# A state-space stage with ScalarE's own softplus, ten products with C on GpSimd in two buffers, and some sums at the next tile's head

## The reference

```python
hs = silu(causal_conv4(x @ W_in_states.T) + conv_b)        # u in the kernel
dt = jax.nn.softplus((hs @ W_dt.T) @ W_dtproj.T + b_dtproj)
Bm, Cm = hs @ W_b.T, hs @ W_c.T
dA  = exp(-exp(A_log)[d, n] * dt[l, d])
dBu = dt[l, d] * Bm[l, n] * hs[l, d]
h[l] = dA[l] * h[l - 1] + dBu[l]                            # a scan along l
y = sum_n h[l, d, n] * Cm[l, n] + hs * D
out = (y * silu(x @ W_in_gates.T)) @ W_out.T
```

## Time and profile before

| | us |
|---|---|
| median of three runs | 3419.03 |
| the runs | 3418.29 to 3426.33 |
| span of the profiled execution | 3415.4 |
| first scan of the state-space stage | 54.54 |
| last product of the stage ends | 1884.6 |
| pitch of a batch, from step 0 to step 0 | 113.7 |

### The profile page before, as it was taken

How to read it: one execution, slowest core, us unless ns; L and a number is a source line. 1 busy time by engine, 2 the same in 40 slices (tenths; PEclk the granted TensorE clock), 3 DMA queues, 4 the chain that set the end, 5 groups by cost and what they waited for, 6 DMA issues and landing times. The chain is left out here.

```text
span 3415.4 us, 47202 instructions
## 1 busy us (share of the span) xinstructions
PE 3074.0 (90%) x16134; PEld 1818.3 (53%) x16134; DVE 2871.5 (84%) x2845; ACT 2597.1 (76%) x5045; POOL 2182.7 (64%) x1332
## 2 busy tenths in 40 slices
PE   7899999999999999999986689989999999879998
PEld 5676667666766676667655334334334433234444
DVE  6999999999999999999989677777777777368887
ACT  5888888888888888888886166666666666757776
POOL 4999999999999999999999233433343342300000
PEclk9999999999999999999998799999999999989999
DMA  4102211221122112211221455455456455131110
GB/s 164 43 30 75 75 45 40 75 75 46 40 75 75 48 37 75 75 49 37 74 90 62 141 150 172 144 170 169 144 174 176 153 166 164 45 112 46 46 44 35
DMA packets 164383, 311.92 MB, mean 91 GB/s; under 512 B 22736, under 2 KB 80208, under 8 KB 164000
## 3 DMA queue, kind: packets, MB, share of 16 engines
q1 hardware_dynamic: 158784, 299.53, 27.7%
q10 hardware_dynamic: 5360, 9.38, 1.1%
HBM read 217.16 MB, written 91.69 MB: 90 GB/s over the span
## 5 line engine op out<-in xcount | busy, mean ns | idle before, releaser
L872 POOL TENSOR_TENSOR bu<-du,bc 128x1024 f32<-128x1024 f32 x512 | 1198.0, 2364 | 88.5 <-DVE states L956 42.7
L736 ACT ACTIVATE states<-dt,negA 128x256 f32<-128x256 f32 x2048 | 850.9, 461 | 221.5 <-DVE hc L969 160.1
L956 DVE TENSOR_TENSOR_SCAN states<-states,bu 128x1024 f32<-128x1024 f32 x416 | 953.2, 2291 | 70.0 <-ACT states L736 63.1
L1608 DVE TENSOR_REDUCE mmax<-s_ps 128x2 f32<-128x1024 f32 x512 | 624.6, 1224 | 248.6 <-PE s_ps L1327 232.0
L1452 ACT ACTIVATE pt<-s_ps 128x512 f32<-128x512 f32 x1024 | 572.4, 596 | 331.9 <-PE s_ps L1336 323.5
L969 DVE TENSOR_TENSOR hc<-states,bc 128x1024 f32<-128x1024 f32 x416 | 509.3, 1224 | 45.8 <-DVE states L956 1.9
L534 PE MATMUL y_ps<-id_sb,hc 128*128 128x128 f32 x3328 | 453.7, 280 | 97.6 <-DVE hc L969 97.6
L534 PEld LDWEIGHTS y_ps<-id_sb,hc 128*128 128x128 f32 x3328 | 382.0, 143 | 255.5 <-DVE hc L969 222.8
L1336 PE MATMUL s_ps<-qst,kst 105*128 105x512 bf16 x1024 | 378.3, 385 | 12.1 <-ACT pt L1452 5.1
L1327 PE MATMUL s_ps<-kst,qst 102*128 102x512 bf16 x1024 | 316.7, 392 | 58.0 <-DMA kst<-mask_d 47.2
L1347 PE MATMUL pv_ps<-pt,vaug 128*32 128x512 f32 x2048 | 274.7, 609 | 12.2 <-ACT o_sb L1493 11.7
(11 more groups left out here) (187 smaller groups left out, 4619.7 us busy)
## 6 DMA issues: line engine op xcount, KB each, us to landing
bc<-bc_scratch SPq DMA_DIRECT2D x128, 512.0 KB, 5.5
stack_d<-parts SPq DMA_DIRECT2D x180, 256.0 KB, 3.0
qst<-stack_d SPq DMA_DIRECT2D x64, 384.0 KB
kst<-stack_d SPq DMA_DIRECT2D x64, 384.0 KB
...
```

The costliest lines, as they stand in the source:

```text
L736: a = act.activation(states[:, bank, first:first + SEQ], dt[:, t, :], ACT.Exp, scale=negA[:, t, c * NS + n:c * NS + n + 1])
L872: pool.tensor_tensor(bu[:, buf, :].rearrange("p (n l) -> p n l", n=NS), du[:, t % (2 * GRP):t % (2 * GRP) + 1, :].to_broadcast([P, NS, SEQ ...
L956: m = dve.tensor_tensor_scan(dst, src, bu[:, BU_OF[k][0], half * 2 * SEQ:(half + n) * 2 * SEQ], 0.0, ALU.mult, ALU.add)
L1608: dve.tensor_reduce(mmax[:, u // HG, c:c + 2], s1_ps[:, pair], AX.X, ALU.max).then_inc(s1_free, 1)
```

## The change

**Softplus.** An evacuation of kind d is now one ACT function, Softplus with the bias, for each of the two tiles, between two table loads. The three log parts go, and so does ACT's wait for `sp_done` before the next group. POOL's part shrinks to du and the memset (`weigh_inputs`), waits for the evacuation itself and comes two steps after it, not five. All other functions of the stage but Silu use the set of Exp.

```diff
-SECOND, THIRD, SOFT = 1, 2, 5
+SOFT = 2
...
-        def softplus(eng, f, par, j):
+        def weigh_inputs(eng, f, par, j):
 
             tiles, step = slice(GRP * j, GRP * j + GRP), slice(j % 2 * GRP, j % 2 * GRP + GRP)
-            dst = dt[:, GRP * j:GRP * j + GRP, :].rearrange("p t l -> p (t l)")
-            eng.wait_ge(sp_poly, f * GROUPS + j + 1)
-            eng.tensor_tensor(sp_t[:, :], sp_t[:, :], sp_e[:, :], ALU.mult)
-            eng.tensor_tensor(dst, dst, sp_l[:, :], ALU.add)
-            eng.drain()
-            eng.tensor_tensor(dst, dst, sp_t[:, :], ALU.add)
-            eng.drain()
+            eng.wait_ge(ev["d"], f * GROUPS + j + 1)
             if j == 0:
                 eng.wait_ge(u_ready, f + 1)
+            eng.drain()
             eng.tensor_tensor(du[:, step, :], dt[:, tiles, :], u[:, par, tiles, :], ALU.mult)
             eng.drain()
-            eng.memset(dt[:, tiles, 0:1], STOP).then_inc(sp_done, 1)
+            eng.memset(dt[:, tiles, 0:1], STOP).then_inc(du_ready, 1)
...
                 elif kind == "d":
-                    if not (isinstance(f, int) and f == 0 and i == 0):
-                        act.wait_ge(sp_done, f * GROUPS + i)
+                    act.preload_act_table_set("softplus")
                     for j in range(GRP):
                         t = GRP * i + j
-                        bias = chan_sb[:, t, C_BDT:C_BDT + 1]
-                        act.activation(sp_e[:, j * SEQ:(j + 1) * SEQ], proj[:, j * SEQ:(j + 1) * SEQ], ACT.Abs, bias=bias)
-                        a = act.activation(dt[:, t, :], proj[:, j * SEQ:(j + 1) * SEQ], ACT.Relu, bias=bias)
+                        a = act.activation(dt[:, t, :], proj[:, j * SEQ:(j + 1) * SEQ], ACT.Softplus,
+                                           bias=chan_sb[:, t, C_BDT:C_BDT + 1])
                     a.then_inc(ev["d"], 1)
+                    act.preload_act_table_set("exp_and_others")
```

```diff
-BUS = 3
+BUS = 4
...
-POOL_STEPS = (0, 5, 12, 20, 24, 28)
+POOL_STEPS = (0, 4, 6, 10, 14, 16, 20, 22, 25, 28)
...
             def times_C(b, k):
-                if k == POOL_STEPS[0]:
+                if k % CPT not in [i % CPT for i in POOL_STEPS[:POOL_STEPS.index(k)]]:
                     pool.wait_ge(c_in[k % CPT], (b + 1) * 16)
                 pool.wait_ge(scan_done, b * STEPS + k + 1)
-                pool.tensor_tensor(hp[:, :], hp[:, :], bc[:, k % CPT, 1, :], ALU.mult).then_inc(hc_pool, 1)
+                h = hp[:, POOL_STEPS.index(k) % 2, :]
+                pool.tensor_tensor(h, h, bc[:, k % CPT, 1, :], ALU.mult).then_inc(hc_pool, 1)
...
-                if k in POOL_STEPS and not (isinstance(b, int) and b == 0 and k == POOL_STEPS[0]):
-                    dve.wait_ge(sum_pool, pool_products(b, k) - 1)
+                if k in POOL_STEPS and pool_products(b, k) > 2:
+                    dve.wait_ge(sum_pool, pool_products(b, k) - 2)
                 for bank, half, n in runs_of(k):
                     src = states[:, bank:bank + n, :].rearrange("p i l -> p (i l)")
-                    dst = hp[:, half * 2 * SEQ:(half + n) * 2 * SEQ] if k in POOL_STEPS else src
+                    dst = hp[:, POOL_STEPS.index(k) % 2, half * 2 * SEQ:(half + n) * 2 * SEQ] if k in POOL_STEPS else src
                     m = dve.tensor_tensor_scan(dst, src, bu[:, BU_OF[k][0], half * 2 * SEQ:(half + n) * 2 * SEQ], 0.0, ALU.mult, ALU.add)
                 m.then_inc(scan_done, 1)
```

```diff
                     for c in range(CPT):
-                        if STEPS - CPT + c in POOL_STEPS:
-                            sp.wait_ge(hc_pool, pool_products(b, STEPS - CPT + c))
-                        else:
-                            sp.wait_ge(hc_dve, products(b, STEPS - CPT + c))
+                        sp.wait_ge(hc_pool, pool_products(b, max(k for k in POOL_STEPS if k % CPT == c or k == 0)))
+                        sp.wait_ge(hc_dve, products(b, max(k for k in DVE_STEPS if k % CPT == c)))
                         spread(c, 1, c_in)
...
                 for k in range(STEPS):
+                    if k % CPT == 0 and k - SUM_AT in POOL_STEPS:
+                        sum_states(b, k - SUM_AT)
...
                     if k not in POOL_STEPS:
                         sum_states(b, k)
-                    if k - SUM_AT in POOL_STEPS:
+                    if k % CPT and k - SUM_AT in POOL_STEPS:
                         sum_states(b, k - SUM_AT)
```

More of the change, by code:

```diff
@@ L527, in sum_states @@
                     pe.wait_ge(hc_pool, pool_products(b, k))
-                    src, done = hp.ap(), sum_pool
+                    src, done = hp[:, POOL_STEPS.index(k) % 2, :], sum_pool
                 else:
@@ L652, in rates @@
             def rates():
[L653 removed]
+                act.preload_act_table_set("exp_and_others")
                 act.activation(negA[:, :, :], chan_sb[:, :, C_ALOG:C_ALOG + STATES], ACT.Exp)
[L655 removed]
                 act.drain()
[L657 removed]
+                act.activation(negA[:, :, :], negA[:, :, :], ACT.Relu, bias=consts[:, 0:1])
                 act.drain()
[L659 to L660 removed]
+                act.activation(negA[:, :, :], negA[:, :, :], ACT.Copy, bias=-RATE_MIN, scale=-1.0).then_inc(negA_ready, 1)
                 act.wait_ge(negA_ready, 1)
@@ L813, in body @@
                             evacuate(bank, kind, i, batch, side)
-                    for j in range(GROUPS):
-                        for start in when(b, k, SP_AT[j]):
-                            if active(start + (j in AHEAD)):
-                                log_part(start + (j in AHEAD), j)
-                        for start in when(b, k, SP_AT[j] + SECOND):
-                            if active(start + (j in AHEAD)):
-                                log_second(j)
-                        for start in when(b, k, SP_AT[j] + THIRD):
-                            if active(start + (j in AHEAD)):
-                                log_third(j)
                     for start in when(b, k, SILU_U):
@@ L904, in body @@
                             if active(start + (j in AHEAD)):
-                                softplus(pool, start + (j in AHEAD), par if (start is b) == (j not in AHEAD) else 1 - par, j)
+                                weigh_inputs(pool, start + (j in AHEAD), par if (start is b) == (j not in AHEAD) else 1 - par, j)
                     if k == W_AT[-1] + 2:
@@ L913, in _ @@
         def _(dve):
-            for i, value in enumerate((SHIFT, -SERIES, REST, 0.0, -RATE_MIN, LOG_SERIES)):
-                dve.memset(consts[:, i:i + 1], value)
+            dve.memset(consts[:, 0:1], -RATE_MIN)
             dve.memset(xpad[:, :, 0:TAPS - 1], 0.0)
@@ L944, in front @@
                 for j in AHEAD:
-                    softplus(dve, 0, 0, j)
+                    weigh_inputs(dve, 0, 0, j)
             def scan(b, k):
```

48 lines of the change are left out of this document (8 added, 40 removed).

## The result

| | before | after |
|---|---|---|
| median of four runs each, same chip, us | 3422.41 | 3365.26 |
| the runs | 3418.29 to 3426.33 | 3361.77 to 3372.34 |
| ratio, with its 95% interval | | 0.984 [0.9825, 0.9855] |
| span of the profiled execution | 3415.4 | 3365.7 |

The account below looks back on a forecast made before the run. DVE's own work was taken to pace the stage, with ACT adding 4.2 us a batch. Gains of 15 batches x 5.2 + 3 (last batch) + 4 (front) = 85 us gave 3334, range 3316 to 3376.

Parts of the forecast that it names:

- DVE waits for sums: Sign of a wrong forecast: DVE waiting for bu or for sums; the forecast put the sums' cost at 0 to 0.1.
- the pitch is over 110: Sign of a wrong forecast: a batch over 110 us or under 107, where 108.5 was forecast.
- rival 1: Engines become tied: half of POOL's wait for DVE adds to DVE's stalls; batch 110.1 us, total 3359; chance 0.17.
- (a): DVE: four more products with C leave it, 5.3 us a batch, all on the path that paces.
- (b): ACT's softplus: clumps of 3.46 us; new stalls at steps 14 and 25, Silu's stay, 4.35 us a batch against 4.2.
- (c): POOL: 106.4 us a batch against about 110, under 108.5; new wait in weigh_inputs for Softplus costed at nothing.
- (d): TensorE: four sums at the heads of steps 8, 12, 16 and 24; hardest is step 16, cost 0 to 0.1.
- at full granted clock: Reading of the ten-batch windows before the change: the engines' busy times were taken at full granted clock.
- (f): The front: chain to the first scan loses some 6 us, but copies of B and C limit the gain to 4.
- (g): Last batch: steps 6 and 10 lose products where DVE then waits for ACT and a projection; gain 3 instead of 5.2.
- Rivals 2 to 4: 2: new stalls don't appear, 3302 (0.08); 3: switches cost more, 3481 (0.07); 4: Softplus at upper bound, 3376 (0.06).

Follow-up runs that it names:

- soft_only: Changed kernel with the old POOL_STEPS table and three buffers of bu, so the new softplus without the ten products: 3413.11 us, ratio 0.9954 to the kernel before.
- no_loads: Changed kernel with Relu in place of Softplus and without its two table loads, so part of the computation is left out: 3329.49 us, measured once.
- step5: Changed kernel with one entry of POOL_STEPS moved, step 4 to step 5: 3364.74 us, ratio 0.9824 to the kernel before.
- after_res: Changed kernel with DVE's residual add issued ahead of scan 0 instead of behind it: 3389.44 us, ratio 0.9904 to the kernel before.
- after_both: Changed kernel with DVE's residual add ahead of scan 0 and ACT's evacuation of s0 in step 2, ahead of the dt group: 3343.43 us, ratio 0.9755.
- moved_front: Changed kernel with POOL_STEPS 4, 14, 25 moved to 5, 12, 26 and the first batch's four gate evacuations in steps 0 to 3: 3338.45 us, ratio 0.9738.
- prod_only: Kernel before with the ten POOL products, sums at the head and two hp buffers, but old softplus and three bu buffers: 3541.11 us, measured once.

## Why the prediction was right, and where not

The time lies in the range, but the working to it does not hold in full, and the prediction's own signs of being wrong were seen: DVE waits for sums, and the pitch is over 110. The time fell inside because the range took in rival 1, whose 3.6 us a batch the gain came to by another cause; that part is luck.

- **(a)** right: 352 products of 1.22 us.
- **(b)** right to 0.15 us a batch. Stalls of 1.18, 0.88, 1.00 and 1.12 us for 1.25, 0.95, 1.0 and 1.15, at the steps named and at no other; steps 3 and 9 show 0.00 and 0.02. Summing ACT's chain and DVE's chain from the same bank release did that. Softplus had the lower bound. The Trainium skill's page ScalarE: Activation LUTs, section What ACT_TABLE_LOAD costs, adds 1.38 us to every switch of set. The trace of after does not agree: 0.7 us of idle time in all before 40 loads behind a Softplus. soft_only and no_loads say the same from the other side.
- **(c)** right in its conclusion. POOL is busy 103.3 a batch for 106.4 forecast, partly since the recorded durations overlap (they add up to 105.4), and bu is there 1.5 us or more before its scan at every step, 3.4 to 8.3 in the median. POOL waits 3.0 a batch for the copies of B and C, 0.9 for scans whose product it makes, and 1.6 for the Softplus ahead of weigh_inputs, up to 1.9 in group 3 of nine of the ten batches. That last is the new wait that (c) named; it lies off the path, as forecast.
- **(d) is the step that failed.** It looked at the four heads that got a new sum and took the hardest, step 16, at 0 to 0.1; there it held. Step 4 gets no sum at its head and was not looked at, though the table puts it into POOL_STEPS. There y comes 1.22 us sooner, and TensorE is behind, for ACT evacuates s0 behind the clump. In place of nothing, DVE waited 1.27 to 3.24 us there, 1.6 a batch, 22 us in all. step5 showed that the missing product is part of it, no_loads that the clump is 0.7 of it, after_res that ACT's order holds the chain, after_both that it is all.
- The clock was no term of the forecast ("at full granted clock"). That reading was right for the mean of ten batches, 1.00, and hid four of 14 with slow matmuls. In after it is part of the 22 us, 0.6 us a time in three batches and 2.0 in one. But the measured 113.7 a batch from which the forecast starts holds 3.3 us of it in 14 batches too.
- **(f)** failed: 1.7 us and the first batch 1.7 longer, for 4. The chain to the first scan was counted without the gate evacuations ahead of decays 0 in ACT's order, and moved_front shows that a front without them wins nothing either.
- **(g)** 3.8 for 3. Right.
- **Rival 1** has the time, 3359, but not by its mechanism: no engine is near its bound, and the half of POOL's wait that it adds is not what is seen. after_both has the same engines as full, and 108.4. Rivals 2 to 4 fall by the stalls, the loads and the Softplus rows.

Left open: the product of step 21 starts 0.46 us after its scan instead of 0.10 in every kernel with the new softplus and ten products (in prod_only that of step 19 does); that is 0.35 us a batch, with no releaser in the trace. And what decides in which batch the clock falls behind the same wait of 1.68 us: in four of 14 batches of before and of after, and in eleven of step5.
